# An attention and mixture-of-experts block: routing in smaller counted steps, weight split without its pause, and DMA transposes for the tokens of batches two to four

## What is computed

```python
x = L0_attn_x
xn = _layernorm(x, axis=-1)
x = x + _L0_attn_ref(xn, Wq, bq, ..., Wo, bo) + _L0_ffn_ref(xn, gate_w, w1, w2)
```

## Time and profile before

| | |
|---|---|
| median of 3 runs | 1560.26 us (1558.79 to 1565.82) |
| the profiled execution's own time | 1556.29 us |
| its span | 1554.5 us |
| PE busy | 1423.9 us (92%) |
| PEld busy | 924.0 us (59%) |
| DVE busy | 1013.7 us (65%) |
| ACT busy | 882.3 us (57%) |
| POOL busy | 566.6 us (36%) |
| DMA, mean | 124 GB/s |
| granted TensorE clock, mean | 0.981 |

### The profile page before, as it was taken

The page is one execution under the profiler, slowest core; times in us unless marked ns, Lnnn a source line. Parts: engine busy times, 40 slices in busy tenths (PEclk is TensorE's granted clock), DMA queues, the critical chain, the costliest instruction groups (busy, mean ns, idle before and its releaser), DMA issues.

```text
span 1554.5 us, 37269 instructions
## 1 busy us (share of the span) xinstructions
PE 1423.9 (92%) x13659; PEld 924.0 (59%) x13659; DVE 1013.7 (65%) x2462; ACT 882.3 (57%) x1994; POOL 566.6 (36%) x595
## 2 busy tenths in 40 slices
PE   4899979998997999989899898999999999999995
PEld 2576656665665666666565566675466556556663
DVE  7887887666878777777788977788343333333331
ACT  5677777665778767776776465777122222222221
POOL 4111232121123213113312233132237777777764
PEclk9999999999999999999999999999999999999998
DMA  7355232433423255453114233145978788888883
GB/s 267 101 141 138 87 108 65 126 102 106 135 85 115 79 150 155 135 157 89 61 61 128 82 105 81 54 150 158 340 152 136 126 133 135 130 143 145 137 131 46
DMA packets 171357, 193.40 MB, mean 124 GB/s; under 512 B 87536, under 2 KB 121072, under 8 KB 171056
## 3 DMA queue, kind: packets, MB, share of 16 engines
q1 hardware_dynamic: 143760, 151.67, 35.6%
q0 software_dynamic: 26128, 37.24, 14.5%
q10 hardware_dynamic: 1296, 2.11, 0.4%
HBM read 93.45 MB, written 53.74 MB: 95 GB/s over the span
## 4 chain that ended last, share of the span: by engine, by line
PE 67%; DVE 11%; issue 7%; ACT 5%; SPq 3%; DMA 3%; POOL 3%; DVEq 0%; ACTq 0%; POOLq 0%
PE S L1240 16%; PE O L1177 7%; PE T L1161 5%; PE S L1150 5%; PE T L1118 4%; PE O L1271 4%; PE M L1271 4%; DVE arena L1544 4%; SPq L993 3%; PE M L1118 3%; PE S L1161 2%; PE M L1161 2%; PE S L1118 2%; PE T L1202 2%; ACT arena L1736 2%
## 5 line engine op out<-in xcount | busy, mean ns | idle before, releaser
L1736 ACT ACTIVATE arena<-arena,mneg 128x1024 f32<-128x1024 f32 (+7 forms) x512 | 395.3, 772 | 72.1 <-DVE mneg L1544 70.4
L1544 DVE CUSTOM_DVE_ANT_0 arena<-S,cF,nsl 128x1024 f32<-128x1024 f32 (+7 forms) x512 | 408.9, 806 | 23.3 <-PE S L1150 14.2
L1240 PE MATMUL S<-arena 128*128 x1704 | 265.6, 312 | 2.0 <-DVE arena L1655 2.0
L1892 POOL DMA_INDIRECT out<-arena x142 | 222.7, 1568 | 105.3 <-issue 43.2
L1150 PE MATMUL S<-arena 96*128 96x512 f16 (+3 forms) x768 | 210.7, 329 | 18.8 <-DVE mneg L1544 17.4
L1240 PEld LDWEIGHTS S<-arena 128*128 128x128 f16 x1704 | 166.3, 98 | 98.2 <-issue 2.8
L1161 PE MATMUL T<-cF,arena 128*128 128x128 f32 x1198 | 199.1, 277 | 24.6 <-DVE arena L1560 13.4
L1177 PE MATMUL O<-arena 128*32 128x128 f32 (+1 forms) x3328 | 176.4, 327 | 13.6 <-DVE arena L1575 13.6
L1753 ACT ACTIVATE arena<-T 128x512 f32<-128x512 f32 (+3 forms) x258 | 118.6, 463 | 109.6 <-PE T L1161 108.7
L1161 PEld LDWEIGHTS T<-cF,arena 128*128 128x128 f32 x1198 | 140.4, 141 | 67.3 <-issue 24.6
L1669 DVE COPY arena<-T 128x512 f16<-128x512 f16 x71 | 30.2, 425 | 213.7 <-PE T L1255 213.7
(11 more groups left out here) (207 smaller groups left out, 2322.5 us busy)
## 6 DMA issues: line engine op xcount, KB each, us to landing
arena<-arena SPq DMA_DIRECT2D x192, 128.0 KB, 2.5
arena<-in_w1T SPq DMA_DIRECT2D x64, 352.0 KB, 3.4
arena<-in_x SPq DMA_DIRECT2D x64, 256.0 KB, 3.4
w_d<-arena SPq DMA_DIRECT2D x32, 352.0 KB, 2.9
arena<-w_d SPq DMA_DIRECT2D x16, 704.0 KB, 6.8
arena<-in_w2T SPq DMA_DIRECT2D x32, 256.0 KB, 2.8
out<-arena SPq DMA_DIRECT2D x32, 256.0 KB, 2.9
xn_d<-arena SPq DMA_DIRECT2D x24, 256.0 KB, 2.0
```

Source lines behind the costliest of these rows:

```text
L1240: tp = pe.matmul(y[:, i * 512:i * 512 + I], xT[:, s % XDEEP, 4 * a + c, :], weights[:, bass.ds(reg[s] + (w_ * NX * W1N + c * 2 * I + i * I ...
L1544: dve.tensor_tensor_reduce(ring[r][:, 0:w], SBK[o.bank["score", u]][:, 0:w], rel[:, S - w:S], nsl[:, hh:hh + 1], 3.0e38, ALU.add, ALU.min, ...
L1736: act.activation(ring[r][:, 0:w], ring[r][:, 0:w], ACT.Exp, bias=mneg[:, m:m + 1], scale=-1.0, accum_out=rs[:, k, c:c + 1]).then_inc(sems[ ...
L1892: pool.indirect_dma_start(out=halves, out_offset=bass.IndirectOffsetOnAxis(row[:, part, s:s + 1].bitcast(U32), 0), in_=yo[:, s % YDEEP, c0 ...
```

## The change

Four edits to the plan, with what each engine does for them:

1. Tokens of batches two to four are transposed by a DMA on SP's queue, from `XH` straight to `xnT`, right behind the store of the same tile. `xtp` and the copy `xt` remain for batch one alone (copy on ACT). The DMA waits for `xnl` and for `v(b-1, 3, 1, 3)`; `xnh` of the buffer's next user waits for the DMA's landing where it waited for `xtp`.
2. The rest of `split_jobs` in units 70 to 105 is gone; a chunk of `w_split` takes 5 units where it took 4.
3. `routing` takes 31 steps up to the lists where it took 14, each with its cost on DVE counted in `load`, which `lighter` reads; the arithmetic is the same.
4. In the lists, `places` is divided in two (`inslot` and `places`), one step apart, and their cost is counted too.

```diff
     def ln_turn(b, half, i):
         add("xnd", b, half, i, sem=f"xnd{half_place(b, half, i)}", inc=16)
+        if b:
+            add("xt", b, half, i, sem=f"xt{half * 4 + i}", inc=16)
+            return
         key = "xtp", b, half, i
...
         def rest():
-            en = lighter(512) if b else "a"
-            add("xt", b, half, i, en, sem="xt" + en)
-            o.count["xt", b, half, i] = o.count["xt", b, half, i, en]
+            add("xt", b, half, i)
             o.give(key, ("xt", b, half, i))
...
             add("wsh", i)
             load["act"] += 0.8
             yield
+            yield
             add("wsl", i)
...
     def routing():
-        add("route", 0)
+        def burst(us, *parts, inc=0):
+            for part in parts:
+                add("route", *part, inc=inc)
+            load["dve"] += us
+
+        burst(0.9, (0, 0), inc=1)
         add("rex")
-        add("route", 1, inc=0)
-        add("route", 2, inc=0)
-        yield
-        for part in (3, 4, 5):
-            add("route", part, inc=0)
+        yield
+        yield
+        burst(1.3, (1, 0))
+        yield
+        for i in range(0, NT, 8):
+            burst(1.2, (2, i))
             yield
-        for part in (6, 7, 8, 9):
-            add("route", part, inc=0)
+        for i in range(0, NT, 4):
+            burst(0.9, (6, i))
             yield
...
-        add("route", 13, inc=0)
-        yield
-        add("route", 14, inc=0)
-        yield
-        add("route", 15)
-        yield
-        add("route", 16)
-        yield
+        for i in range(-1, 5):
+            burst(0.6, (13, i))
+            if i % 2 == 0:
+                yield
+        burst(0.9, (14, 0))
+        yield
+        burst(1.3, (14, 1))
+        yield
+        burst(1.3, (14, 2))
+        yield
+        for i in range(2):
+            burst(0.9, (15, 2 * i))
+            yield
+            burst(1.2, (15, 2 * i + 1), inc=i)
+            yield
+        burst(1.5, (16, 0))
+        yield
+        burst(0.6, (16, 1), inc=1)
         yield
         for c in range(NT // 4):
+            add("inslot", c)
+            add("slots", c)
+            load["dve"] += 0.7
+            yield
             add("places", c)
-            add("slots", c)
+            load["dve"] += 1.2
             yield
...
-        if u >= 4 and not (u < 128 * (B - 1) and 70 <= u % 128 < 106):
+        if u >= 4:
             while split_jobs and next(split_jobs[0], jobs) is jobs:
...
+            elif kind == "xt" and key[0]:
+                b, half, i = key
+                tt = half * 4 + i
+                on.wait_ge(*at("xnl", *key))
+                on.wait_ge(*at("v", b - 1, NG - 1, 1, 3))
+                sp.dma_start_transpose(xnT[:, :, :, tt * P:(tt + 1) * P].rearrange("p a c n -> p (a c) n"),
+                                       XH[half_place(*key)]).then_inc(at(*step)[0], 16)
...
                 if half_before(*key):
-                    on.wait_ge(*at("xtp", *half_before(*key)))
+                    on.wait_ge(*at("xt" if half_before(*key)[0] else "xtp", *half_before(*key)))
                     on.wait_ge(*at("xnd", *half_before(*key)))
```

More of the change, by code:

```diff
@@ L1310, in bc, with route @@
             return x.unsqueeze(axis).to_broadcast(shape)
-        def route(part):
+        def route(part, i):
             if part == 0:
@@ L1317, in route @@
                 for half in range(2):
[L1318 to L1321, removed]
+                    for t in range(4):
+                        on.wait_ge(*at("xnl", B - 1, half, t))
+                        on.wait_ge(*at("xt", B - 1, half, t))
+                        on.wait_ge(*at("xnd", B - 1, half, t))
                 then(dve.tensor_reduce(mx, logits[:, :, :], AX, ALU.max))
@@ L1328, in route @@
                 then(dve.tensor_tensor(pr, pr, bc(mx, 2, SH), ALU.mult))
[L1329 to L1332, removed]
+            elif part == 2:
+                for t in range(i, i + 8):
+                    ins = dve.max(m8[:, t, :], pr[:, t, :])
+                if i == NT - 8:
                     then(ins)
[L1334 to L1337, removed]
+            elif part == 6:
+                for t in range(i, i + 4):
+                    ins = dve.max_index(idx[:, t, :], m8[:, t, :], pr[:, t, :])
+                if i == NT - 4:
                     then(ins)
@@ new lines, in route @@
+                then(dve.tensor_tensor(c0, c0, bc(bt, 1, SH), ALU.add))
+                then(dve.tensor_tensor(c0, c0, m8, ALU.add))
+            elif part == 15 and i % 2 == 0:
+                oh = (oh0, oh1)[i // 2]
+                then(dve.tensor_tensor(oh, oh, c0, ALU.mult))
+                then(dve.tensor_reduce(mx, oh, AX, ALU.add))
+            elif part == 15:
+                k = i // 2
+                then(dve.tensor_copy(ti32, mx))
+                then(dve.tensor_scalar(pos, ti32, P - 1, None, ALU.bitwise_and))
+                then(dve.tensor_scalar(ti32, ti32, 7, None, ALU.logical_shift_right))
+                then(dve.tensor_copy(posf[:, k, :], pos))
+                then(dve.tensor_copy(slf[:, k, :], ti32))
+                ins = dve.scalar_tensor_tensor(pair[:, k, :, 0], tokid[:, 0:NT], -float(NT * P), posf[:, k, :],
+                                               ALU.add, ALU.subtract)
+                if k == 0:
+                    then(ins)
+                else:
+                    ins.then_inc(sems["route"], 1)
+                    on.wait_ge(*at("route", 15, 3))
+            else:
@@ L1689, in scalar @@
                 act.dma_start(xn_d[t * P:(t + 1) * P, :], XH[half_place(*key)]).then_inc(at(*step)[0], 16)
-            elif kind == "xt" and key[3] == "a":
-                b, half, i, _ = key
+            elif kind == "xt" and not key[0]:
+                b, half, i = key
                 tt = half * 4 + i
@@ L1858, in gpsimd @@
                 i, t = chunk(c)
-                on.wait_ge(sems["inslot"], c + 1)
+                on.wait_ge(*at("inslot", c))
                 one = ohs[:, :, 0, :]
```

103 lines of the change are left out of this document (43 added, 60 removed).

## The result

The changed kernel is slower: over 19 runs each, a median of 1574.85 us (1567.18 to 1581.15) against 1566.50 us (1558.79 to 1572.77) for the kernel before, a ratio of 1.0056, 95% interval 1.0039 to 1.0073. I had forecast 1539 us in 1524 to 1560, faster with a chance of 0.75. The profiled execution took 1569.62 us, its span 1567.8 us, 13.3 us more than before. One profile is one execution: units 0 to 71 of batch one, whose steps are the same in all kernels here, took 129.0 to 134.8 us in the thirteen profiles, so a difference of some 6 us between whole batches says little by itself, and the units in which it arises are looked at.

The account below looks back on a forecast made before the run. It took PE to bound the attention for 92% of 1041 us; terms -13 + 1 + 6 - 2 - 3 - 10 = -21 us took the profiled 1556.3 us to 1535.3, plus 4.0 for a median: 1539 us, range 1524 to 1560.

Parts of the forecast that it names:

- split without a pause: Units 70 to 105, batches one to three: added split work on DVE costs +6 us (bounds 0 and 14).
- that sign: Predicted mark in the new profile: units 88 to 95 of batch one near 15 us.
- late transposes: Rival, layer norm stretches: ACT's xnh waits six times for DMA landings, up to 40.5 us; 1578 us, chance 0.09.
- The stall in batch two: The eight units of 25.1 us in batch two: reduction moves to unit 116 of batch one, -3 us (+1 to -6).
- Transposes, what goes: Units 72 to 103: 192 PE transposes and their copies go, -13 us of at most 16.9.
- rival of the clock: Rival: less PE work lowers the granted clock in three stretches, 2.7 us each; 1547 us, chance 0.09.
- What comes: 24 DMA transposes on SP's queue: late starts of xnh for tile 3, +1 us net (0 to 5).
- What is given back: Batch four: the split ends earlier, so 14 of 18 chunks leave it, -2 us (0 to -5).
- Routing: Batch four's routing and lists in small steps: shorter DVE chains hold PE less, -10 us (-3 to -17).
- rival of amount: Rival, routing: the same 30 us of DVE work cost the same in pieces; 1549 us, chance 0.11.
- full DVE: Rival, units 70 to 105: DVE becomes the limit and lays half the split's work bare; 1559 us, chance 0.13.

Follow-up runs that it names:

- e4: The kernel before with only the transposes of batches two to four by DMA; 0.9954 of the kernel before, median 1559.87 us.
- e2: The changed kernel with transposes back on PE and their copies on ACT and DVE; 1.0037 of the kernel before, median 1571.39 us.
- e1: The changed kernel with the split's pause in units 70 to 105 and 4 units a chunk back; 0.9835 of the kernel before, median 1540.56 us.
- e5: The changed kernel without 18 of the 56 w_max loads, those in units 70 to 105 of batch one; 0.9989 of the kernel before, median 1561.53 us.
- e7: The changed kernel with five steps in place of one behind the reduction on POOL; 1.0149 of the kernel before, median 1590.51 us.
- e9: The changed kernel with 4 units a chunk of w_split, still without a pause; 1.0044 of the kernel before, median 1571.29 us.
- e8: e1 with five steps in place of one behind the reduction on POOL; 0.9797 of the kernel before, median 1533.05 us.
- e10: e8 without its DMA transposes; 0.9792 of the kernel before, median 1534.58 us.
- e11: e8 with each tile's DMA transpose ahead of its store on SP's queue; 0.9787 of the kernel before, median 1533.07 us.
- e3: The kernel before with only the new routing in 31 steps and the lists in two; 0.9864 of the kernel before, median 1546.44 us.

## Why the prediction was wrong

The step that failed is **split without a pause**, and in it the ground for the price. I took DVE's busy time for the limit and put +6 us; units 72 to 103 took 223.3 us in the changed kernel against 197.3 in e4, +26 us (+24 us in e2, with no DMA transpose in play). DVE did not fill. Units 88 to 95 of batch one did take 15.1 us where I had 15, but DVE was busy for 13.0 of them, so that sign came true for another reason. What I left out is SP's queue: I had written that "the split's loads and stores now in the same queue" spoke for the late transposes, and put 0.09 on that rival, but priced it from landings alone, with L between 3 and 11 us from the issue. The landings stayed near what the rows said (4.0 us in the median, 3.4 in e1). It was the issue that came 4.5 us late, because a load in front of it waits for a reduction. I did count the transposes' 1.23 us on SP, not the waits of what stands before them; e5 shows what the loads cost by leaving them out.

The other terms:

- **The stall in batch two**, forecast -3 us: its move cost 10.3 us in units 112 to 127, and nothing came back in 24 to 31, since a store behind the stacks took its place. I saw DVE's wait and not what else POOL makes there. The 5.6 us of "issue" ahead of the reduction were in the earlier trace rows; the gap behind it I had not looked for.
- **Transposes, what goes**, forecast -13 us: -4.1 us (e4). The way was right and the size wrong by three. The bound of 16.9 us "by PE alone" was itself too high, since transposes overlap what follows them: 11.8 us could go. Three quarters was read off PE's busy share; but in a stretch with pauses, PE's busy time follows the clock, and the clock fell, which took 6.8 us. My rival of the clock had that way and that size (8 us); the error was to set it against the forecast where both came true together.
- **What comes**, +1 us: right where the queue is free (1.4 and 1.5 us in e1 and e4), 11.2 us without the pause.
- **What is given back** in batch four, -2 us: 246.7 against 248.4 us in e1, of that size, but too little to be told from what single profiles differ by.
- **Routing**, forecast -10 us: batch four won 18.2 us (266.6 in e4, 248.4 in e1). Units 8 to 15 take 16.7 us, PE has no wait above 1.5 us in the batch, its clock is 1.00. I had left 7 us for new small stalls and old ones that stay; they did not come. The rival of amount falls; which part of the new `routing()` won it is open.
- The kernel before measured 1566.5 us over 19 runs where three had given 1560.26; I had added 4.0 us to the profile's time and 10 would have been right. By itself this would not have taken the forecast out of its range.

Added up by place, the change is +21.9 us in units 72 to 103 of the three batches (+26.0 less the 4.1 of the transposes), +10.3 in units 112 to 127 of batch one, -0.2 in the stall of batch two and -19.0 in batch four: +13.0, against 13.3 us of the span.

The full DVE, the rival with the largest chance, fell in e5. The late transposes had 1578 us, near what was measured, but that nearness is chance: L stayed short, ACT waited 11.2 us for landings and not 40, and e2 is nearly as slow with no DMA transpose at all.

Left open: what POOL does in the gaps around the reduction; which part of the routing's edit won its time; whether missing work or moved pauses lowered the clock in e4; and how much of the split's 0.7% is the loads and how much the stores, which was not taken apart.

## What to carry to other kernels

A queue that waits in order is a resource of its own: before work is moved into a stretch, list what stands in the DMA queue there with the waits of each entry, not only its busy time. A job that shares a queue with a burst (here twelve stacks in 8.45 us) should be placed by where its entries fall among the burst's: moving it by a few steps moved the stall (e7, e9), it did not remove it. Long chains of small operations cut into counted and spread steps were worth 1.4%; transposes taken off a PE that pauses were worth at most 0.5%: of their 16.9 us in flight 5.1 overlapped other matmuls, and a lower clock took back 6.8. Before pricing work that goes, take its rows out of the union of the engine's busy time, not the busy time of its line alone.

## What the runs showed of the hardware

- A partition reduction of 0.37 us on POOL comes with two gaps in which POOL waits for nothing that the profile shows: 5.5 to 6.4 us ahead of it, and 7.0 to 8.4 us before the first `TENSOR_TENSOR` after it, in all thirteen kernels. In e8, e10 and e11 a `CAST` in between started without a gap.
- With 64 PE transposes fewer in each of three stretches of 66 us, TensorE was at its lower level for 34.1 to 41.0 us (e1, e4, e8, e11) where it had been for 17.1 to 23.9 us (before, e3, e10), though idle time grew by about 1 us in e4.
- Token stores of 256 KB landed in 2.0 us in the median with the pause and PE transposes (before, e3, e10), in 2.6 to 2.7 us with a DMA transpose right behind each (e1, e4, e8), in 3.4 us without the pause but with PE transposes (e2), and in 3.7 us in the changed kernel, without the pause and with DMA transposes. So most of the rise in the changed kernel came with the missing pause, not with the transposes.
